# Issuing the experts' down-projection weights from ScalarE's DMA queue

## The chip, the cores and the metric

The kernel runs on one core of a Trainium2 chip. The metric is device time in microseconds (us) of one execution. Times of the kernel before are the median of three runs, and one further execution was taken with the hardware profiler; its rows stand below.

Engines are named as the profile names them: PE is TensorE's matmuls, PEld its weight loads, DVE is VectorE, ACT is ScalarE, POOL is GpSimd, SP is SyncE, which only issues transfers. A "q" behind an engine (SPq, ACTq) is its sequencer, where DMA issues are recorded. Among the DMA queues, q1 carries what SP issues, q10 what ACT issues and q0 what POOL issues.

## What is computed

One decoder layer on 4096 tokens of width 512, in float32: a Mamba-2 mixer, cross attention to a context of 77 rows, then a slot mixture of experts. Its feed-forward part is what this change touches. Each of 16 experts works on its own slot row, 2 rows (one per sequence):

```
h = layernorm(o)                       # o: 16 slot rows per sequence, from attention over x
u = silu(einsum('besd,edf->besf', h, W1) + b1)      # W1: 16 x 512 x 2048
g = silu(einsum('besd,edf->besf', h, Wg) + bg)      # Wg: 16 x 512 x 2048
y = einsum('besf,efd->besd', u * g, W2) + b2        # W2: 16 x 2048 x 512
o = o + y
out = mha(x, o, o, ...)                # the combine stage, over all tokens
```

So each expert needs three matrices of 4 MB, 12 MB in all, for very little arithmetic, and 16 experts need 201 MB.

## The kernel before

The program has three large parts: the token stages (mixer, cross attention, attention of slots to tokens), the expert stage, and the combine stage. The parts are separated by who needs what; the expert stage is a loop over 16 experts, `experts(eng, body)`, which every engine runs for itself: experts 0 and 1 written out, a hardware loop over experts 2 to 13 in steps of two, experts 14 and 15 written out. Engines meet only by semaphores.

**Units and ring.** The weights of one expert are cut into 6 units of 2 MB: units 0 and 1 are W1, 2 and 3 are Wg (these four are the up projections' units), 4 and 5 are W2 (the down projections' units). They land in a ring of 6 slots in SBUF, all of 128 partitions x 4096 floats. `slot_of(unit, e)` gives the slot; from expert 2 on, a unit takes the slot that the same unit of the expert before had. The units of expert 0 are fetched during the token stages from ACT's queue, units 0 to 2 of expert 1 go to three spare places at the end of the token stages, so 87 units are left for the expert stage. (In this text "(e,u)" is unit u of expert e.)

**A W1 or Wg unit** is copied as 128 rows of 16 KB, **a W2 unit** as 256 rows of 8 KB (`fetch_unit`, L839 and L842).

**Who waits for what.** PE's `expert` runs, for w = 0 (W1) and 1 (Wg): 16 matmuls on each of two units (L1538), then bias matmuls (L1545). ACT's `activate` takes the silu of each (L1583), DVE multiplies them (L1574), PE transposes the product (L1550), DVE copies it (L1577), and PE runs the down projection on units 4 and 5 (L1560). PE waits for `ring_in` of the unit's slot, and when its last matmul on a unit is done it counts `unit_used` of the slot up (`release`). SP's `stream` waits for `unit_used` of the slot and issues the next unit for it. SP does this in the order 0, 1, 2, 3, 4, 5 of each expert:

```
for unit in range(UNITS):
    if isinstance(e, int) and e == 1 and unit < EXTRA:
        continue
    slot = slot_of(unit, e)
    sp.wait_ge(unit_used[slot], uses(unit, e))
    fetch_unit(sp, io, ring[:, slot, :], ring_in[slot], e, unit)
```

After the last expert's units SP waits for unit (15,0) to be used and issues three loads of 512 KB for the combine stage into its slot (L1871 twice, L1876), rows of 2 KB. POOL issues two bias loads of 8 KB per expert. After the last down projection a chain of small matmuls and copies makes the combine stage's matrices, all engines meet in a barrier, and the combine stage starts at 1430.7 us of the span.

Of the kernel before, what the change touches and what calls it, by code (L numbers as in the profile page):

```python
# [48 lines left out]
UNITS = 6  # L49
# [3 lines left out]
def broadcast(ap, shape):  # L53
    return ap.broadcast_to(shape)
# [89 lines left out]
def wait_later(eng, sem, value):  # L144

    if not isinstance(value, int) or value > 0:
        eng.wait_ge(sem, value)
# [686 lines left out]
def fetch_unit(sp, io, dst, arrived, e, unit):  # L834

    kind, half = unit // 2, unit % 2
    if kind < 2:
        src = (io["e_W1"], io["e_Wg"])[kind].rearrange("e (p k) f -> e p (k f)", p=P)[bass.ds(e, 1), :, half * UNIT:(half + 1) * UNIT]
        sp.dma_start(dst, src.rearrange("o p f -> (o p) f")).then_inc(arrived, 16)  # L839
    else:  # L840
        src = io["e_W2"].rearrange("e (q p s) n -> e p q (s n)", q=4, p=P)[bass.ds(e, 1), :, 2 * half:2 * half + 2, :]
        sp.dma_start(dst.rearrange("p (q n) -> p q n", q=2), src.rearrange("o p q n -> (o p) q n")).then_inc(arrived, 16)  # L842
# [10 lines left out]
def tokens_stage(nc, io, hold, ring, ring_in):  # L853
    with Stage(nc, "mix", hold["arena"], PROJ1_AT) as mt:
        hold["banks"] = mt.banks(4)
        hold["score_banks"] = mt.stack.enter_context(nc.psum_tensor("mix_scores", [P, HG, 512], F32))
        first = mixer_parts(nc, io, hold, mt)
        with Stage(nc, "crs") as st, Stage(nc, "exp") as et:
            slots = expert_parts(nc, io, hold, ring, ring_in, et)
            cross_rows(nc, io, hold, ring, ring_in, st, first, slots)  # L860
# [586 lines left out]
def expert_parts(nc, io, hold, ring, ring_in, st):  # L1447
# [29 lines left out]
    slot, dbo, ln_g, ln_b = (rows[:, i, :] for i in range(4))  # L1477
# [19 lines left out]
    unit_used = [st.sem(f"unit_used{i}") for i in range(UNITS)]  # L1497
# [3 lines left out]
    def slot_of(unit, e):  # L1501

        return unit if isinstance(e, int) and e == 0 else (unit + UNITS - EXTRA) % UNITS

    def uses(unit, e):

        return e - 1 if unit < EXTRA and not (isinstance(e, int) and e == 0) else e
# [71 lines left out]
    def activate(act, e):  # L1579
        wait_later(act, s["gu_done"], e)  # L1580
        for w, dst in ((0, up), (1, gate)):
            act.wait_ge(s["up_done"], 2 * e + w + 1)
            nc.scalar.activation(dst[:], bank[w][:], ACT.Silu).then_inc(s["silu_done"], 1)  # L1583

    def experts(eng, body):

        for e in (0, 1):
            body(e, e, 0)
        with eng.Fori(1, EXPERTS // 2 - 1) as i:
            for u in (0, 1):  # L1590
                body(2 * i + u, u, i)
        for e in (EXPERTS - 2, EXPERTS - 1):
            body(e, e % 2, e // 2)
# [4 lines left out]
    def fetch_rows(sp):  # L1598
        sp.dma_start(dbv[:], io["d_bv"]).then_inc(s["dbv_in"], 16)
        sp.dma_start(rows, io["slot_rows"][:, 0:4, :]).then_inc(s["rows_in"], 16)  # L1600
        sp.dma_start(b2, io["slot_rows"][:, 4, :]).then_inc(s["rows_in"], 16)

    def stream(sp):
        def combine_weights(dst, src, layout):
            sp.dma_start(dst[:], src.rearrange(layout, p=P)).then_inc(s["comb_w_in"], 16)

        for dst, src in ((cbk, io["c_bk"]), (cbv, io["c_bv"]), (cbq, io["c_bq"])):
            sp.dma_start(dst[:], src).then_inc(s["comb_w_in"], 16)
        sp.wait_ge(s["zn_turned"], BATCH * SM)
        combine_weights(cwo, io["c_Wo"], "(k p) n -> p k n")  # L1610
        sp.wait_ge(s["ao_done"], 1)
        combine_weights(cwk, io["c_Wk"], "(p k) n -> p k n")
        combine_weights(cwv, io["c_Wv"], "(p k) n -> p k n")
        sp.wait_ge(s["wo_done"], 1)
        combine_weights(cwqT, io["c_WqT"], "(k p) n -> p k n")

        def step(e, u, half):
            if isinstance(e, int) and e == 0:
                return
            for unit in range(UNITS):  # L1620
                if isinstance(e, int) and e == 1 and unit < EXTRA:
                    continue
                slot = slot_of(unit, e)
                sp.wait_ge(unit_used[slot], uses(unit, e))
                fetch_unit(sp, io, ring[:, slot, :], ring_in[slot], e, unit)
            if isinstance(e, int) and e == 1:
                sp.dma_start(cbo[:], broadcast(io["c_bo"].rearrange("(o n) -> o n", o=1), [P, D])).then_inc(s["comb_w_in"], 16)
        experts(sp, step)

        sp.wait_ge(unit_used[slot_of(0, EXPERTS - 1)], EXPERTS - 1)  # L1630
        fetch_turned(sp, io, hold, 0, 0)
        fetch_turned(sp, io, hold, 1, 1)
        fetch_tokens(sp, io, hold, 0, 0)
# [126 lines left out]
                                 ACT.Copy).then_inc(s["znT_done"], 1)  # L1760

    def activate_all(act):
        experts(act, lambda e, u, half: activate(act, e))
        act.wait_ge(s["k4_done"], 1)
        nc.scalar.activation(k4[:], bank[6][:], ACT.Copy).then_inc(s["k4_out"], 1)
        for k in range(KC):
            act.wait_ge(s["m2_done"], k + 1)
            nc.scalar.activation(hold["m2"][:, :, k, :].rearrange("p b (g r) -> p g b r", g=GROUPS),
                                 bank[k][:].rearrange("p (g b r) -> p g b r", g=GROUPS, b=BATCH), ACT.Copy).then_inc(s["m2_out"], 1)
        act.wait_ge(s["kb_done"], 1)  # L1770
        nc.scalar.activation(hold["kb2"][:].rearrange("p b g r -> p g b r"), bank[6][:].rearrange("p (g b r) -> p g b r", g=GROUPS, b=BATCH),
                             ACT.Copy, scale=SCALE).then_inc(s["m2_out"], 1)
# [10 lines left out]
    def normalise(dve):  # L1783
# [71 lines left out]
        for i in range(BATCH * SM):  # L1855
# [3 lines left out]
                                           ALU.mult, ALU.add).then_inc(s["vo_out"], 1)  # L1859

    return dict(fetch_extra=fetch_extra, fetch_rows=fetch_rows, stream=stream, constants=constants, biases=biases, turn_tokens=turn_tokens,
                multiply=multiply, take_tokens=take_tokens, activate=activate_all, invert_sums=invert_sums, divide_tokens=divide_tokens,
                normalise=normalise, keep_busy=keep_busy)

# [4 lines left out]
def fetch_turned(sp, io, hold, i, u):  # L1869

    sp.dma_start(hold["x2T"][u][:].rearrange("p t k n -> p t (k n)"),  # L1871
                 io["x2T"].rearrange("(t p) n -> p t n", p=P)[:, bass.ds(i * T2, T2), :]).then_inc(hold["x2T_in"][u], 16)


def fetch_tokens(sp, io, hold, i, u):
    sp.dma_start(hold["x2"][u][:], io["x2"].rearrange("(t p) n -> p t n", p=P)[:, bass.ds(i * T2, T2), :]).then_inc(hold["x2_in"][u], 16)  # L1876
# [322 lines left out]
```

## Time and profile before

| | us |
|---|---|
| median of 3 runs | 1575.49 (1572.14 to 1576.46) |
| the profiled execution, its own time | 1573.41 |
| its span in the trace | 1571.8 |
| expert stage in the span | 964.4 to 1410.8 |
| PE busy over the whole span | 1376.2 (88%) |
| DVE, ACT, POOL busy | 803.4, 449.4, 235.4 |

The profile is of one execution. The time of that execution is 1.6 us above its span. Busy time of PE counts matmuls in flight, also when they are spread thinly; in the expert stage the engine-by-engine busy shares are low except for the DMA engines.

### The profile page before, as it was taken

How to read it: one execution, taken by the hardware profiler on the slowest of the kernel's cores; microseconds unless marked ns; L12 is line 12 of the kernel's file. 1: busy time of each engine (PE TensorE's matmuls, PEld its weight loads, DVE VectorE, ACT ScalarE, POOL GpSimd, SP SyncE). 2: the span in 40 equal slices, each digit the busy share in tenths (PEclk: the TensorE clock that was granted, in tenths of full speed). 3: DMA queues.
4: the chain of work that ended last, by engine and by line, in shares of the span. 5: the costliest groups of instructions: out<-in, count | busy, mean ns of one | idle time of the engine just before them, and what ended most of it. 6: DMA issues, size and time to landing. Idle time of an engine off the chain costs nothing. (4 is left out here: it accounts for less than half of the span.)

```text
span 1571.8 us, 26619 instructions
## 1 busy us (share of the span) xinstructions
PE 1376.2 (88%) x10011; PEld 866.8 (55%) x10011; DVE 803.4 (51%) x2195; ACT 449.4 (29%) x938; POOL 235.4 (15%) x214
## 2 busy tenths in 40 slices
PE   6899999999999999999999989856666666678996
PEld 3777777777677777777777755211111111126663
DVE  0646676767777676767676753000000000004997
ACT  2434434334144444444444431000000000002332
POOL 1111111011022121212222221000000000001221
PEclk9899999999999999999999999998988998889998
DMA  9342233122211421153111156999999999972663
GB/s 355 122 147 80 69 95 95 53 82 81 81 56 61 158 105 58 43 192 125 47 53 47 47 210 265 415 426 424 427 426 423 426 427 424 426 298 68 201 201 134
DMA packets 75259, 309.28 MB, mean 197 GB/s; under 512 B 9692, under 2 KB 14940, under 8 KB 57513
## 3 DMA queue, kind: packets, MB, share of 16 engines
q1 hardware_dynamic: 71720, 293.23, 48.5%
q10 hardware_dynamic: 2432, 14.68, 2.7%
q8 instruction: 53, 0.87, 0.2%
q0 software_dynamic: 1024, 0.27, 0.1%
q14 instruction: 30, 0.24, 0.1%
HBM read 274.33 MB, written 33.82 MB: 196 GB/s over the span
## 5 line engine op out<-in xcount | busy, mean ns | idle before, releaser
L1538 PE MATMUL mix_scores<-all_ring,all_space 128*32 128x512 f32 x976 | 146.0, 709 | 102.1 <-DMA all_ring<-in_e_W 53.9
L1574 DVE TENSOR_TENSOR all_space<-all_space 128x512 f32<-128x512 f32 x16 | 11.1, 694 | 396.6 <-ACT all_space L1583 396.6
L175 PE MATMUL mix_bank<-all_ring,all_space 128*128 128x256 f32 x672 | 156.8, 387 | 2.1 <-POOL all_ring L1419 2.1
L1538 PEld LDWEIGHTS mix_scores<-all_ring,all_space 128*32 128x32 f32 x976 | 29.9, 118 | 205.2 <-DMA all_ring<-in_e_Wg 79.2
L175 PEld LDWEIGHTS mix_bank<-all_ring,all_space 128*128 128x128 f32 x672 | 126.6, 192 | 28.6 <-issue 9.0
L1583 ACT ACTIVATE all_space<-mix_scores 128x512 f32<-128x512 f32 x32 | 19.1, 597 | 428.7 <-PE mix_scores L1545 428.7
L1151 POOL TENSOR_TENSOR all_space<-all_space 128x1232 f32<-128x1232 f32 x32 | 72.2, 2257 | 396.4 <-DVE all_space L1113 396.4
L1560 PE MATMUL mix_scores<-all_ring,all_space 128*32 128x512 f32 x512 | 114.6, 657 | 15.7 <-DVE all_space L1577 12.6
L930 PE MATMUL mix_bank<-all_space 128*128 128x128 f32 x1024 | 119.8, 275 | 0.0
L969 PE MATMUL mix_bank<-all_space 128*128 128x512 f32 x256 | 117.6, 603 | 0.8 <-ACT all_space L1034 0.8
L930 PEld LDWEIGHTS mix_bank<-all_space 128*128 128x128 f32 x1024 | 116.9, 192 | 0.7 <-issue 0.5
L245 DVE SCALAR_TENSOR_TENSOR all_ring<-all_ring,all_space 128x256 f32<-128x256 f32 x192 | 84.4, 482 | 53.0 <-ACT all_ring L194 50.4
L756 PE MATMUL mix_scores<-all_space,all_ring 128*128 128x512 f32 x240 | 105.5, 592 | 0.8 <-DVE all_ring L806 0.8
L1080 DVE TENSOR_REDUCE all_space<-mix_scores 128x16 f32<-128x1232 f32 x30 | 43.3, 1442 | 93.8 <-PE mix_scores L943 93.8
L1560 PEld LDWEIGHTS mix_scores<-all_ring,all_space 128*32 128x32 f32 x512 | 27.6, 119 | 91.1 <-issue 66.1
L756 PEld LDWEIGHTS mix_scores<-all_space,all_ring 128*128 128x128 f32 x240 | 45.5, 190 | 52.0 <-issue 50.2
L969 PEld LDWEIGHTS mix_bank<-all_space 128*128 128x128 f32 x256 | 47.0, 194 | 48.5 <-issue 48.4
L1028 ACT ACTIVATE all_space<-all_space 128x1232 f32<-128x1232 f32 x32 | 39.4, 1231 | 113.0 <-DVE all_space L1082 113.0
L950 PEld LDWEIGHTS mix_scores<-all_ident,all_space 128*77 128x77 f32 x512 | 58.2, 148 | 18.6 <-issue 15.4
L1052 ACT ACTIVATE all_space<-mix_scores 77x512 f32<-77x512 f32 x128 | 65.3, 588 | 7.1 <-PE mix_scores L950 6.7
L228 POOL TENSOR_TENSOR all_ring<-all_ring,all_dwv 128x512 f32<-128x512 f32 x24 | 30.5, 1272 | 243.8 <-ACT all_dwv L214 242.5
L1058 ACT ACTIVATE all_space<-all_space 128x512 f32<-128x512 f32 x32 | 26.1, 816 | 143.1 <-DVE all_space L641 143.1
(282 smaller groups left out, 2292.0 us busy)
## 6 DMA issues: line engine op xcount, KB each, us to landing
all_ring<-in_e_W SPq DMA_DIRECT2D x58, 2048.0 KB, 26.3
all_ring<-in_e_Wg SPq DMA_DIRECT2D x29, 2048.0 KB, 27.3
all_ring<-in_xT SPq DMA_DIRECT2D x8, 1024.0 KB, 7.7
all_ring<-scratch_rates SPq DMA_DIRECT2D x64, 128.0 KB, 4.2
all_z<-in_x SPq DMA_DIRECT2D x16, 512.0 KB, 4.5
all_space<-scratch_x SPq DMA_DIRECT2D x32, 256.0 KB, 2.8
scratch_x<-all_space SPq DMA_DIRECT2D x32, 256.0 KB, 2.0
scratch_x2T<-all_space SPq DMA_DIRECT2D x32, 256.0 KB, 2.0
```

Source lines behind the costliest of these rows:

```text
L175: last = nc.tensor.matmul(bank[:, i * BT:(i + 1) * BT], hold["win"][:, k, m * P:(m + 1) * P], hold["xT"][b % 2][:, k, :], start=(k == 0), ...
L245: last = nc.vector.scalar_tensor_tensor(conv[:, m0 + i, :], proj[:, m0 + i, k:k + BT], taps[:, m0 + i, k:k + 1], conv[:, m0 + i, :], ALU.m ...
L756: last = nc.tensor.matmul(outputs(c)[b], yT[:, b, g * P:(g + 1) * P], wout[:, g, :], start=(g == 0), stop=(g == GROUPS - 1))
L930: last = nc.tensor.matmul(AV[:, g * P:(g + 1) * P], wq[:, k, g * P:(g + 1) * P], x1T[:, k, :], start=(k == 0), stop=(k == KC - 1))
L950: last = nc.tensor.transpose(SC[0:CTX, g, h * P:(h + 1) * P], pr[:, h * GROUPS + g, :], hold["ident"][:])
L969: last = nc.tensor.matmul(TO[:], yT[:, k, :], wo[:, k, :], start=(k == 0), stop=(k == KC - 1))
L1028: nc.scalar.activation(pr[:], pr[:], ACT.Exp, scale=SCALE).then_inc(s["exp_done"], 1)
L1052: nc.scalar.activation(prT[:, g * HG:(g + 1) * HG, :].rearrange("p h t -> p (h t)"), SC[0:CTX, g, :], ACT.Copy).then_inc(s["prT_done"], 1)
L1080: nc.vector.tensor_reduce(top[:].rearrange("p (i h) -> p i h", i=HG), src, AX.X, ALU.max).then_inc(s["top_done"], 1)
L1151: nc.gpsimd.tensor_tensor(pr[:], pr[:], broadcast(rden[:].unsqueeze(2), [P, HEADS, CTX]), ALU.mult).then_inc(s["normed"], 1)
L1538: last = nc.tensor.matmul(bank[w][q * ROWS:(q + 1) * ROWS, :], hm[u][:, k, :], weights[:, at:at + FQ], start=(k == 0), stop=False)
L1560: last = nc.tensor.matmul(bank[3][q * ROWS:(q + 1) * ROWS, :], guT[:, i, q * ROWS:(q + 1) * ROWS], weights[:, (j * 4 + i) * D:(j * 4 + i + ...
```

## The change

The loop over a unit's wait and fetch becomes a helper, `refill`, that any issuing engine can call. SP's stream now issues units 0 to 3 of each expert from 1 on. Units 4 and 5 of each expert from 1 on are issued by ACT, at the start of its step for that expert, ahead of its waits for the silu. Nothing else moves; the waits on `unit_used`, the slots and the sizes are the same.

```
+    def refill(eng, e, unit):
+        slot = slot_of(unit, e)
+        eng.wait_ge(unit_used[slot], uses(unit, e))
+        fetch_unit(eng, io, ring[:, slot, :], ring_in[slot], e, unit)
+
     def stream(sp):
...
-            for unit in range(UNITS):
+            for unit in range(UNITS - 2):
                 if isinstance(e, int) and e == 1 and unit < EXTRA:
                     continue
-                slot = slot_of(unit, e)
-                sp.wait_ge(unit_used[slot], uses(unit, e))
-                fetch_unit(sp, io, ring[:, slot, :], ring_in[slot], e, unit)
+                refill(sp, e, unit)
...
     def activate_all(act):
-        experts(act, lambda e, u, half: activate(act, e))
+        def step(e, u, half):
+            if not (isinstance(e, int) and e == 0):
+                for unit in (UNITS - 2, UNITS - 1):
+                    refill(act, e, unit)
+            activate(act, e)
+        experts(act, step)
```

On SP, this is one piece of the difference, the end of the second expert's step in the loop over experts 2 to 13. `exp_unit_used1` and `exp_unit_used2` are the slots of units 4 and 5.

```order
 L839 DMA all_ring<-in_e_Wg 128x4096 [waits exp_unit_used5]
 L839 DMA all_ring<-in_e_Wg 128x4096 [waits exp_unit_used0]
-L842 DMA all_ring<-in_e_W 128x2x2048 [waits exp_unit_used1]
-L842 ISA [waits exp_unit_used2]
-L842 DMA all_ring<-in_e_W 128x2x2048
 L1589 REGISTER_ALU
 L1589 COMPARE_AND_BRANCH
```

SP goes from unit 3 of one expert straight to unit 0 of the next, and no longer waits for the down projection's slots.

On ACT, this is the step of expert 0, the step of expert 1 and the start of the loop. Semaphores are printed by the name of their first owner: `tab_tables_ready` is here `up_done` (PE has finished an up projection) and `tab_rates_turned` is `gu_done` (DVE has multiplied).

```order
 L1583 ACTIVATE all_space<-mix_scores 128x512 [waits tab_tables_ready] x2
+L842 DMA all_ring<-in_e_W 128x2x2048 [waits exp_unit_used1]
+L842 DMA all_ring<-in_e_W 128x2x2048 [waits exp_unit_used2]
 L1583 ACTIVATE all_space<-mix_scores 128x512 [waits tab_tables_ready,tab_rates_turned]
 L1583 ACTIVATE all_space<-mix_scores 128x512 [waits tab_tables_ready]
 L1589 UNCONDITIONAL_BRANCH
 L1589 ISA
+L842 ISA [waits exp_unit_used1]
+L842 DMA all_ring<-in_e_W 128x2x2048
+L842 ISA [waits exp_unit_used2]
+L842 DMA all_ring<-in_e_W 128x2x2048
```

ACT's two issues for an expert stand between the second silu of the expert before and the first silu of its own.

## Rows read from the trace of the kernel before

**Rows 1.** The page's slices, 39.3 us each: PE and DMA busy, GB/s.
```profile
PE   6899999999999999999999989856666666678996
DMA  9342233122211421153111156999999999972663
GB/s 355 122 147 80 69 95 95 53 82 81 81 56 61 158 105 58 43 192 125 47 53 47 47 210 265 415 426 424 427 426 423 426 427 424 426 298 68 201 201 134
```

**Rows 2.** Busy time by stretch: the full stage, and three stretches at its end.
```profile
core 0: us, PE busy (x) PEld busy (x) DVE busy (x) ACT busy (x) POOL busy (x), PEclk, DMA share, GB/s
1000.00:1390.00 390.00, 259.87 (x1544) 64.76 (x1538) 22.84 (x50) 15.53 (x26) 13.02 (x25) 0.89 1.01 425
1403.00:1407.00 4.00, 4.00 (x12) 0.94 (x14) 0.00 (x0) 0.00 (x0) 0.00 (x0) 0.59 0.15 58
1407.00:1411.00 4.00, 4.00 (x24) 1.10 (x20) 0.14 (x1) 0.00 (x0) 0.11 (x1) 1.00 0.06 22
```

**Rows 3.** Waits between 1000 and 1360 us: total, times, longest.
```profile
PEld mix_scores L1538 <- DMA all_ring<-in_e_Wg: 67.1, 23, 3.9
PEld mix_scores L1538 <- DMA all_ring<-in_e_W: 56.8, 17, 3.9
PEld mix_scores L1560 <- DMA all_ring<-in_e_W: 8.9, 10, 2.1
```

**Rows 4.** DMA issues: count, KB each, median us from issue to landing.
```profile
all_ring<-in_e_W SPq DMA_DIRECT2D x58, 2048.0 KB, 26.3
all_ring<-in_e_Wg SPq DMA_DIRECT2D x29, 2048.0 KB, 27.3
```

**Rows 5.** Timeline, an expert in mid-stage at reduced clock: start, duration, engine, line.
```profile
1337.53 3.20 PE L1538 MATMUL mix_scores<-all_ring,all_space 128*32 128x512 f32 x16 [2.97 <-DMA all_ring<-in_e_Wg]
...
1344.99 7.00 PE L1560 MATMUL mix_scores<-all_ring,all_space 128*32 128x512 f32 x32 [0.79 <-DVE all_space L1577]
...
1350.27 2.13 SPq L842 DMA_DIRECT2D all_ring<-in_e_W  x2
```

**Rows 6.** Timeline, an expert near the start, at full clock.
```profile
1035.89 1.92 PE L1538 MATMUL mix_scores<-all_ring,all_space 128*32 128x512 f32 x16 [2.97 <-DMA all_ring<-in_e_Wg]
...
1041.66 3.63 PE L1560 MATMUL mix_scores<-all_ring,all_space 128*32 128x512 f32 x16 [0.78 <-DVE all_space L1577]
...
1045.32 5.33 SPq L842 DMA_DIRECT2D all_ring<-in_e_W  x2
```

**Rows 7.** Timeline, the last expert: unit 3 arrives, down projection, what follows.
```profile
1397.21 1.92 PE L1538 MATMUL mix_scores<-all_ring,all_space 128*32 128x512 f32 x16 [1.61 <-DMA all_ring<-in_e_Wg]
...
1402.98 7.84 PE L1560 MATMUL mix_scores<-all_ring,all_space 128*32 128x512 f32 x32 [0.79 <-DVE all_space L1577]
...
1407.19 0.14 PEld L1560 LDWEIGHTS mix_scores<-all_ring,all_space 128*32 128x32 f32 x6 [0.29 <-DMA all_ring<-in_e_W]
...
1410.75 0.49 PE L1714 MATMUL mix_bank<-all_ident,all_space 128*128 128x128 f32 x2
```

**Rows 8.** DMA view of 547 to 549 us: queue, packets, MB, share.
```profile
DMA packets 87, 0.81 MB, mean 404 GB/s; under 512 B 0, under 2 KB 0, under 8 KB 43
q10 hardware_dynamic: 44, 0.72, 98.0%
q1 hardware_dynamic: 43, 0.09, 11.2%
```

**Rows 9.** The same view of 706 to 708 us.
```profile
DMA packets 161, 0.85 MB, mean 426 GB/s; under 512 B 0, under 2 KB 0, under 8 KB 76
q10 hardware_dynamic: 85, 0.70, 82.4%
q1 hardware_dynamic: 76, 0.16, 19.9%
```

**Rows 10.** Timeline, the start of the expert stage: PE, ACT's silu, SP's issues.
```profile
964.39 3.64 PE L1538 MATMUL mix_scores<-all_ring,all_space 128*32 128x512 f32 x32 [0.39 <-DVE all_space L1830]
966.38 0.33 SPq L839 DMA_DIRECT2D all_ring<-in_e_Wg  x1
968.09 2.95 SPq L842 DMA_DIRECT2D all_ring<-in_e_W  x2
971.09 0.48 SPq L1627 DMA_DIRECT2D all_space<-in_c_bo  x1
972.53 9.48 SPq L839 DMA_DIRECT2D all_ring<-in_e_W  x2
973.25 0.60 ACT L1583 ACTIVATE all_space<-mix_scores 128x512 f32<-128x512 f32 x1 [3.69 <-PE mix_scores L1545]
983.25 8.06 SPq L839 DMA_DIRECT2D all_ring<-in_e_Wg  x2
```

**Rows 11.** Issues at L842 on ACT's queue, duration in ns and where.
```profile
L842 ACTq DMA_DIRECT2D all_ring<-in_e_W x2: 381/383/385, 701.3 to 717.1; - x2
```

## The prediction, made before the changed kernel ran

> **What bounds the kernel now.** I read the page's slices first [rows 1]. In most of the span PE is busy in nine tenths of a slice and the DMA engines in one to four. From slice 26 to 35 it is the other way round: PE falls to five to eight tenths, the DMA engines stand at nine or more, and the rate is flat at 415 to 427 GB/s. That is the expert stage, the only place the change touches. The view by stretches says the same more sharply [rows 2]: from 1000 to 1390 us the 16 DMA engines are busy for 1.01 of the time at 425 GB/s, at a mean granted PE clock of 0.89. So a 2 MB unit takes 2.097 MB / 425 GB/s = 4.93 us, one expert 29.6 us. The waits show who pays [rows 3]: PE's weight loads wait 67.1 + 56.8 us for W1 and Wg units, and only 8.9 us for W2 units. A unit lands 26 to 27 us after its issue [rows 4], over five unit times, so five to six units are always queued. The queue never runs dry and is served in order, so inside the stage a unit arrives every 4.93 us whatever PE does. The stage's length is its bytes over 425 GB/s, plus what follows the last arrivals.
>
> What follows is in [rows 7]. Unit (15,3) starts PE at 1397.21. Silu, multiply and transposes take until 1402.98, 5.77 us, and the two down units another 7.84 us. Unit (15,5), the last one, is there when PE comes to it at 1407.19 (idle before it 0.29 us). So the end of the stage, 1410.75, is **the arrival of unit 3 plus 13.6 us**; the time in which units 4 and 5 arrive is hidden in that chain. Beside this, the DMA rate at the very end is 58 and then 22 GB/s [rows 2], a share of 0.15 and 0.06, about one engine of 16. One engine runs some 8 us behind the others, and landings go by the last one. It moves the same bytes in both kernels, so I treat it as the clock of the stage.
>
> **The change part by part.** (1) Issue cost: 30 issues leave SP and come to ACT, at 0.38 us each [rows 11]. SP had nothing to do but wait. ACT was idle for most of the stage (15.53 us busy of 390 [rows 2]). Its two issues for an expert wait for slots that the down projection before frees, and PE runs the next up projection only after that, at least 2 x 1.92 us [rows 6] before ACT's silu is wanted. So the silu queued behind the waits is not late: 0. If that cover were gone, it would be 2 x 0.38 us for each of 15 experts, 11 us.
>
> (2) Bytes: the same, at the same 425 GB/s as long as one queue has work. 0, with bounds below.
>
> (3) **Order of arrival: the term that counts.** Before, one queue served 0, 1, 2, 3, 4, 5. Now there are two. How do they share an engine? The token stages show it, where ACT fetched expert 0's units beside SP's 2 KB rows. From 547 to 549 us q10 moved 44 packets (0.72 MB, 16 KB each) and q1 43 packets (0.09 MB, 2 KB each) [rows 8]; from 706 to 708 us, with W2's 8 KB packets, 85 against 76 [rows 9]. So they alternate packet by packet, whatever a packet holds. A W1 or Wg unit gives each engine 8 packets of 16 KB, 4.93 / 8 = 0.616 us each; a W2 unit 16 packets of 8 KB, 0.308 us each. A pair takes 0.924 us, SP gets two thirds of the bytes and ACT one third. SP carries 4 of 6 units, so the two queues use exactly their shares: 32 pairs are 29.6 us, one expert.
>
> Now let x be the W2 packets (of the 32 of its expert) that an engine still has to move when unit 3 has landed. In the kernel before x is 32, units 4 and 5 whole, 9.86 us. In the changed one x shrinks, as W2 is moved beside Wg. The last expert's unit 3 then lands x times 0.308 us before the end of the bytes instead of 9.86 us before it. What bounds x? From below: ACT can issue unit 4 of an expert only when half of the down projection before is done. By the rows that is 9.4 us after unit 3 came to PE at full clock [rows 6] and 12.7 us at reduced clock [rows 5], and I allow 0.9 us more until data moves (my choice; no row shows it). If ACT's queue is just never dry, the leftover is worked off in that time: x = 10.3 / 0.924 = 11 to 13.6 / 0.924 = 15. From above: unit 5 lands x times 0.924 us after unit 3, then PE needs 3.63 us for its half of the down projection, 2 us for unit 0 of the next expert, and 1 us passes to SP's issue; this must fit in 29.6 us for SP's queue to stay filled, so x is at most 24. Between 15 and 24 nothing pulls x either way, so the start decides.
>
> The start [rows 10]: SP issued (1,3), (1,4), (1,5) at 966.4, 968.1 and about 970.6. Now ACT issues (1,4) only after expert 0's second silu ends, 973.85. SP sends (1,3), then (2,0) at 972.5. ACT's queue starts 5 us late, is alone for about 2 us near 981 (SP waits for the down projection's slots), ends (1,5) near 999.5, and has moved only some 6 of expert 2's 32 packets when (2,3) lands near 1005. So x starts at about 26, is pushed under 24 by SP's full ring, and should stay near the top. I take x = 20: unit (15,3) lands 20 x 0.308 = 6.2 us before the end of the bytes instead of 9.86, **+3.7 us**. With x from 15 to 24 it is +5.2 to +2.5.
>
> (4) With a large x, PE gets to the next up projection late. For x = 20 unit 5 lands at 18.5, its half ends at 22.4, and four units back to back (964.39 to 973.2, 8.8 us [rows 10]) end at 31.2, against 29.6 plus the 2.9 us that PE spends on unit 3 and the biases when its arrival decides: no loss at full clock. For x = 24 it is 34.9 against 32.5, +2.4. At a clock of 0.89 a little more. I put **+0.5** (0 to 2.4); it grows as (3) shrinks, so the sum of the two stays between 3.6 and 5.5.
>
> (5) Start gap: between the end of (1,3) near 972 (with 0.7 us of the small load behind it) and the first data of (2,0) near 973.4 the engines stand almost idle, where before (1,4) followed. **+0.5 us** (0 to 1).
>
> (6) At the end SP's three loads of 512 KB now share the engines with units (15,4) and (15,5): packets of 2 KB, about 0.09 us. Twenty W2 packets then take 20 x 0.40 = 8 us after unit 3, and the second half of the down projection wants unit 5 at 10 us (1407.19 - 1397.2 [rows 7]): 0, and 0 for the combine stage, whose first loads land before its start at 1430.7.
>
> Sum: 3.7 + 0.5 + 0.5 = **+4.7 us**. The profiled execution took 1573.41 us (span 1571.8); with the change it would take 1578.1. The median of the runs shown is 2.1 us above the profiled one, so the prediction against it is 1575.5 + 4.7 = 1580.2 us.
>
> **Rivals.**
> - *Even sharing by bytes.* If long packets are cut or taken in bursts, ACT gets half while both have work. Both W2 units then land with or before unit 3, x is between 0 and 11, and unit (15,3) lands 0 to 3.4 us before the end of the bytes: +6.4 to +9.9, with the start gap about +8.7, 1584 us. Against it stand [rows 8] and [rows 9], where packet counts match and bytes don't. The Trainium skill (DMA: Bandwidth & Descriptors, "Queues, rings and completion order") says an engine drains a whole packet of some 9 to 17 descriptors before it turns to the next ring; if a turn were so long, a turn would be a unit's whole share on either queue, which is this rival. The packets in this trace are single rows, so I hold it for the less likely.
> - *Two streams cost rate.* Two places of HBM read in turn, one engine already lagging. 1% of 434 us of streaming is +4.3 on top, 1584.5. For it: 404 GB/s in [rows 8]; against it: that is beside 2 KB packets, and [rows 9] shows 426.
> - *Two streams gain rate (the other side).* If an engine overlaps one ring's packet with the other's, each packet may cost less. 425 would have to become 430 to pay the 4.7 us back; 435 would give -10 + 4.7 = -5.5, 1570 us. Against it: the share is 1.01 already [rows 2], and in the mixed stretches the sum of both queues is 404 to 426, never above [rows 8, 9]. The same page of the Trainium skill ("Issuing engines are not separate DMA queues") says that spreading issues over engines saves only sequencer time; no run here shows it yet for two large streams.
> - *Nothing moves that can be measured.* x stays at its top, PE is not late, and the lagging engine's tail hides the rest: +2 to +3, 1578 us.
>
> **How the numbers follow.** About 0.3%, 4.7 us, is what a measurement of this kernel can tell from no change; my likeliest case lies on that line. Packet sharing as worked out (sum 3.6 to 6.5): 0.58. Even bytes 0.10, lost rate 0.12, gained rate 0.08, nothing that shows 0.12. Of the likeliest case somewhat over half counts as slower, with the two dearer rivals 0.53; the rest of it, the fourth rival and half of the gain make 0.40 the same; 0.07 faster. The likeliest case's own range is 1578.5 to 1582. For eight in ten I go from 1574.5 (part of the gained rate) to 1586.5 (the dear rivals with the 1 to 2 us by which runs differ).
>
> **What would show it.** In mid-stage: the two queues' packet counts equal, 425 GB/s and share 1.01 as before; W2 units about 30 us from issue to landing at most; PE waiting for W2 units (L1560) as well as for W1 and Wg; unit 5 landing 14 to 22 us after unit 3. At the end: the last expert's L1538 on unit 3 starts 3 to 5 us later than 1397.2, and L1714 follows it by 13.6 us as before. The even-bytes rival would show no waits at L1560 and unit 3 as the last to land. It is wrong if the rate in the stage differs by 1% either way, if ACT's issues last much over 0.38 us (a full queue) and delay its silu, or if the end of the stage no longer hangs on unit 3.

## The result, and the profile after

The change made the kernel slower, by well under 1%. Four runs gave a median of 1585.24 us (1583.03 to 1589.16), against 1574.9 us before (1572.14 to 1576.46); the ratio (after over before) is 1.0067, 95% interval 1.0053 to 1.008. Timed again later on another occasion, seven runs gave 1585.11 us against 1576.14 us, ratio 1.0057 (1.0036 to 1.0078). So the loss is 9 to 10 us where I forecast 4.7. The direction held, and the measured 1585.24 us lies in the range of 1574.5 to 1586.5; the forecast size was half of the measured one.

The profiled execution took 1589.16 us (span 1587.6), 3.9 us above the median. The page's slices, as in [rows 1], with the granted clock added:

```profile
PE   6899999999999999999999989776676677678996
PEclk9899999999999999999999999987888878878999
DMA  9342233222211421152111058999999999952553
GB/s 345 131 143 83 65 94 94 69 65 81 87 54 55 166 94 59 53 207 95 59 40 59 34 207 309 423 425 427 424 425 426 425 420 414 428 213 66 199 199 133
```

The stage is still flat at the DMA engines' rate. The page's DMA queues and issues, answering to [rows 4]:

```profile
q1 hardware_dynamic: 63560, 230.31, 38.6%
q10 hardware_dynamic: 10592, 77.60, 12.3%
...
all_ring<-in_e_W ACTq DMA_DIRECT2D x34, 2048.0 KB, 18.6
all_ring<-in_e_Wg SPq DMA_DIRECT2D x29, 2048.0 KB, 26.2
```

The view by stretches, answering to [rows 2]:

```profile
core 0: us, PE busy (x) PEld busy (x) DVE busy (x) ACT busy (x) POOL busy (x), PEclk, DMA share, GB/s
1000.00:1360.00 360.00, 253.47 (x1408) 67.27 (x1404) 21.45 (x48) 14.33 (x24) 13.00 (x25) 0.83 1.01 424
1421.40:1444.70 23.30, 18.03 (x101) 12.07 (x99) 6.73 (x15) 3.66 (x7) 0.99 (x2) 0.85 0.00 1
```

The first row is the middle of the stage: the same share and nearly the same rate (425 before), but a PE clock of 0.83 where the same stretch had 0.89. The second is the chain behind the last down projection. In the first profile of before it looks like this:

```profile
1411.00:1430.70 19.70, 14.43 (x98) 9.97 (x98) 6.60 (x15) 3.63 (x7) 0.88 (x2) 0.99 0.00 1
```

The same work took 3.3 us longer at the lower clock. The waits between 1000 and 1360 us, answering to [rows 3]:

```profile
PEld mix_scores L1560 <- DMA all_ring<-in_e_W: 50.4, 12, 6.5
PEld mix_scores L1538 <- DMA all_ring<-in_e_Wg: 49.7, 12, 6.3
```

PE now waits once per expert for unit 3 (L1538) and once for unit 5 (L1560), and no longer for units 0 to 2. The timeline of the last two experts, answering to [rows 5] and [rows 7]:

```profile
1377.27 3.47 PE L1538 MATMUL mix_scores<-all_ring,all_space 128*32 128x512 f32 x16 [3.44 <-DMA all_ring<-in_e_Wg]
...
1384.58 3.63 PE L1560 MATMUL mix_scores<-all_ring,all_space 128*32 128x512 f32 x16 [0.79 <-DVE all_space L1577]
1388.25 10.52 ACTq L842 DMA_DIRECT2D all_ring<-in_e_W  x2
...
1392.03 4.49 PE L1560 MATMUL mix_scores<-all_ring,all_space 128*32 128x512 f32 x10 [3.82 <-DMA all_ring<-in_e_W]
...
1407.00 2.97 PE L1538 MATMUL mix_scores<-all_ring,all_space 128*32 128x512 f32 x16 [2.64 <-DMA all_ring<-in_e_Wg]
1409.72 1.76 PE L1545 MATMUL mix_scores<-all_space 128*32 128x512 f32 x8
...
1414.46 7.05 PE L1560 MATMUL mix_scores<-all_ring,all_space 128*32 128x512 f32 x32 [0.79 <-DVE all_space L1577]
1421.44 0.49 PE L1717 MATMUL mix_bank<-all_ident,all_space 128*128 128x128 f32 x2
...
1424.83 1.94 PE L1728 MATMUL mix_bank<-all_dwv,all_space 128*32 128x512 f32 x8 [0.47 <-DVE all_space L1851]
```

Read it so: PE starts on (14,3) at 1377.27 and on (14,5) only at 1392.03, 14.8 us later, and behind that it runs the next expert's units, which have landed meanwhile, back to back. In the following I call such a stretch of several units in a row a burst. L1728 takes 1.94 us here; the same eight matmuls took 1.06 us in the first profile of before (L1725 there), so they ran at about half speed.

**Where the time went.** This execution reached the expert stage 4.9 us later than the first one of before (969.25 against 964.39), ahead of anything the change touches; the next profile of the same program began it at 960.96. So I count from the stage's first L1538. Two profiles of the changed kernel and three of the kernel before (the later ones are told of below) give:

| us | before, three profiles | changed, two profiles | difference of means |
|---|---|---|---|
| first L1538 to PE's start on (15,3) | 432.8, 432.6, 432.5 | 437.8, 439.2 | +5.9 |
| from there to the end of the last down projection | 13.5, 13.4, 13.4 | 14.4, 14.9 | +1.2 |
| from there to the combine stage's first matmul | 19.95, 19.96, 22.88 | 23.23, 23.15 | +2.3 |
| combine stage | 141.1, 141.0, 142.7 | 142.9, 142.9 | +1.3 |

In all +10.7 us, in keeping with 9 to 10 in the medians. The first line is the arrival of the last unit that the up projections need. In the other three, 4.8 us, PE waits for no weight unit in the changed kernel; they are the same instructions at a lower PE clock. Below, "+439.2" means 439.2 us after the stage's first L1538, and "the chain" is the third line.

### The profile page after: what moved, and what is told of

It reads as the page before. It is cut to its first block and busy times, and to the rows that moved or that the text cites. A ratio compares the mean times of both kernels' runs of the same rounds, so it can differ in the third digit from the quotient of the medians.

```text
span 1587.6 us, 26633 instructions
## 1 busy us (share of the span) xinstructions
PE 1404.1 (88%) x10011; PEld 881.1 (56%) x10011; DVE 804.0 (51%) x2195; ACT 450.3 (28%) x938; POOL 235.1 (15%) x214
## 5 line engine op out<-in xcount | busy, mean ns | idle before, releaser
L1538 PE MATMUL mix_scores<-all_ring,all_space 128*32 128x512 f32 x976 | 171.6, 685 | 45.7 <-DMA all_ring<-in_e_Wg 45.3
L1560 PE MATMUL mix_scores<-all_ring,all_space 128*32 128x512 f32 x512 | 151.5, 764 | 59.4 <-DMA all_ring<-in_e_W 46.8
L1560 PEld LDWEIGHTS mix_scores<-all_ring,all_space 128*32 128x32 f32 x512 | 32.9, 135 | 165.0 <-issue 89.9
L930 PE MATMUL mix_bank<-all_space 128*128 128x128 f32 x1024 | 119.8, 275 | 0.0
L1538 PEld LDWEIGHTS mix_scores<-all_ring,all_space 128*32 128x32 f32 x976 | 39.1, 119 | 129.2 <-issue 68.6
L1028 ACT ACTIVATE all_space<-all_space 128x1232 f32<-128x1232 f32 x32 | 39.3, 1230 | 113.8 <-DVE all_space L1082 113.8
L998 PE MATMUL mix_bank<-all_space 128*128 128x128 f32 x512 | 67.3, 285 | 0.1
```

The source lines that it names most:

```text
L930: last = nc.tensor.matmul(AV[:, g * P:(g + 1) * P], wq[:, k, g * P:(g + 1) * P], x1T[:, k, :], start=(k == 0), stop=(k == KC - 1))
L998: last = nc.tensor.matmul(slot_bank(t)[:, m * P:(m + 1) * P], hold["m1"][:, k, m * P:(m + 1) * P], x2T[u][:, k, :], start=(k == 0), stop=( ...
L1538: last = nc.tensor.matmul(bank[w][q * ROWS:(q + 1) * ROWS, :], hm[u][:, k, :], weights[:, at:at + FQ], start=(k == 0), stop=False)
L1560: last = nc.tensor.matmul(bank[3][q * ROWS:(q + 1) * ROWS, :], guT[:, i, q * ROWS:(q + 1) * ROWS], weights[:, (j * 4 + i) * D:(j * 4 + i + ...
```

## The experiments

Each ratio is against the median of the kernel before, timed on the same occasion.

**The changed kernel again.** No edit.

> The changed kernel as it is, timed again with a second profile. Reading of the first profile: unit (15,3) reaches PE 4.9 us later after the start of the expert stage (437.8 instead of 432.8 us), and PE's clock is lower around and behind the end of the stage, which costs another 4 to 6 us. Theory A (arrival order and clock are both systematic): unit 3 again 4 to 6 us later counted from the stage's first L1538, the clock over the span 0.940 to 0.945 against about 0.957, the stretch from the last down projection's end to the combine stage's first L1927 again 2 to 4 us longer than 19.9 us, time 9 to 11 us above the kernel before. Theory B (only the order is systematic, the clock was this execution's chance): unit 3 the same 5 us later, clock back at 0.955, time 4 to 6 us above.

Measured: 1585.11 us, ratio 1.0057 (1.0036 to 1.0078), the clock over the span 0.943 in the median of its runs, 0.954 in those of the kernel before. (15,3) came at +439.2 us, the stretch behind the down projection took 23.15 us. Theory A: both parts come again.

**The last expert's W2 back on SP.**

```
-            for unit in range(UNITS - 2):
+            last = isinstance(e, int) and e == EXPERTS - 1
+            for unit in range(UNITS if last else UNITS - 2):
...
-            if not (isinstance(e, int) and e == 0):
+            if not (isinstance(e, int) and e in (0, EXPERTS - 1)):
```

> The changed kernel, but the last expert's units 4 and 5 are issued by SP behind its unit 3, as before; experts 1 to 14 keep both queues. If the late arrival of (15,3) is the order of arrival alone, it reaches PE 432 to 434 us after the stage's first L1538 instead of 437.8, and the time falls by 4 to 5 us against the changed kernel. If what costs is something in the steady state of two queues (rate, start gap), it stays at 437 to 438. The clock in the stage should stay at the changed kernel's 0.84 in both theories, since the PE bursts of experts 2 to 14 are as in the changed kernel; if the clock is what is left, the time is still 4 to 6 us above the kernel before.

Measured: 1577.6 us, ratio 1.0012 (0.9996 to 1.0028), so 7.5 us of the changed kernel's 9 came back, by the place of two transfers out of 30. (15,3) was no longer waited for, since PE came to it late: (14,5) is still late (PE starts on it at 1387.84 us of the span), and PE runs four units back to back behind it, as step (4) of the prediction describes for a large x. The transposes began 441.0 us after the first L1538, 4.0 later than before and 3.6 earlier than the mean of the two changed profiles; the down projection then ran without a stop and ended at 448.3, 4.8 us before the mean of the two changed profiles. The chain behind it took 19.96 us, at a mean clock of 0.98, though the middle of the stage stood at 0.83:

```profile
1000.00:1360.00 360.00, 246.79 (x1396) 65.64 (x1398) 21.44 (x48) 14.33 (x24) 12.98 (x25) 0.83 1.01 422
```

But the spells at low clock had not gone, they had moved: the combine stage took 144.3 us here, more than the 141.0 to 142.9 of the five profiles in the table. Chain and combine stage together are 164.3 us, against 166.2 and 166.0 in the changed kernel and 161.1, 161.0 and 165.6 in the kernel before.

So the order of arrival in the last expert is what costs most: of the 7.5 us, 4.8 are the earlier end of the stage and some 1.8 the clock behind it. The clock in mid-stage doesn't decide the clock of the chain. My expectation for this run was 4 to 5 us of gain, which is what the end of the stage gave; I had not counted the clock that comes back with it.

**Rows of 4 KB for W1 and Wg, on two queues and on one.** These two and the next two runs copy other rows of the same matrices, so each expert multiplies permuted weights; bytes, units, waits and instruction counts stay.

```
-        src = (...)[kind].rearrange("e (p k) f -> e p (k f)", p=P)[bass.ds(e, 1), :, half * UNIT:(half + 1) * UNIT]
-        sp.dma_start(dst, src.rearrange("o p f -> (o p) f")).then_inc(arrived, 16)
+        src = (...)[kind].rearrange("e (k p) (c n) -> e p c k n", p=P, c=2)[bass.ds(e, 1), :, half, :, :]
+        sp.dma_start(dst.rearrange("p (k n) -> p k n", k=4), src.rearrange("o p k n -> (o p) k n")).then_inc(arrived, 16)
```

> The changed kernel with W1 and Wg units copied as 512 rows of 4 KB from other places of the matrix (so the numbers that the experts multiply are permuted; sizes, counts and waits are the same). Theory packets (an engine alternates packet by packet): a pair is 4 KB for SP and 8 KB for ACT, ACT gets two thirds while both have work, W2 units land in some 7 to 12 us, PE no longer waits at L1560, and unit 3 is the last to land: unit (15,3) reaches PE 9 to 11 us later than in the kernel before (442 to 444 us after the stage's first L1538), so some 4 to 5 us slower than the changed kernel, if 4 KB packets cost no rate. Theory bytes (both queues share bytes evenly): nothing changes against the changed kernel, 437 to 439 us.

> The kernel before with W1 and Wg units as 512 rows of 4 KB (operands permuted): partner of the earlier 4 KB run with two queues, where unit (15,3) reached PE 454.9 us after the stage's first L1538, 22 us later than in the kernel before. Theory packets: 10 us of that are the order (all of W2 landed before unit 3) and 12 us are the rate of 4 KB packets; here, on one queue, unit (15,3) comes at 443 to 446 and the bytes end at 453 to 455, time 10 to 13 us above the kernel before. Theory bytes: the order is worth only 5 us there as well, so the rate must be 17 us, and unit 3 comes at 449 to 451 here.

Measured: on two queues 1602.18 us (ratio 1.0166, 1.0142 to 1.0191) with (15,3) at +454.9; on one queue 1591.78 us (1.0094, 1.0078 to 1.011) with (15,3) at +445.4. The order is worth 9.5 us here, as the theory of packets says; the bytes theory wanted 5. The time, however, fell 17 us behind the changed kernel instead of 4 to 5, since 4 KB rows cost 12 us in themselves (413 GB/s in mid-stage on one queue, 164 ns a packet). The one-queue run was 15 us above the kernel before where I had 10 to 13: its chain took 23.09 us and its combine stage 142.9, although PE takes the units there as they land. The DMA view of 8 us of the two-queue run, in which both queues have work:

```profile
q10 hardware_dynamic: 283, 2.18, 65.4%
q1 hardware_dynamic: 283, 1.16, 36.2%
```

283 packets each, and two thirds of the engines' time for ACT's larger ones. Equal counts alone don't say how many packets an engine takes from one queue before it turns. The end of the changed kernel's first profile does, from 1410.9 to 1412.4 us, where ACT's 8 KB rows run beside SP's 2 KB rows:

```profile
DMA packets 8, 0.04 MB, mean 27 GB/s; under 512 B 0, under 2 KB 0, under 8 KB 4
q10 hardware_dynamic: 4, 0.03, 5.2%
q1 hardware_dynamic: 4, 0.01, 1.4%
```

A share of 6.6% is one engine of 16, and in the packet records its eight packets alternate, one row of ACT and one of SP every 0.39 us. So a turn is one row. In the 4 KB run with two queues PE no longer waited at L1560, only for unit 3 (waits between 1000 and 1360 us):

```profile
PE mix_scores L1538 <- DMA all_ring<-in_e_Wg: 126.9, 17, 12.0
```

**Rows of 8 KB, on two queues and on one.** As above with `"e (c k p) n -> e p c k n"` and k=2, so that all packets are alike.

> The changed kernel with W1 and Wg units copied as 256 rows of 8 KB, as W2's are (so the numbers that the experts multiply are permuted). To be read against the next run, which has the same rows on one queue. Theory packets: both queues' packets are 8 KB, so they share evenly while both have work, few W2 packets are left when unit 3 has landed (0 to 12), and unit (15,3) reaches PE 7 to 11 us later after the stage's first L1538 than in its one-queue partner (16 KB rows: 4.9 and 6.4 us in two profiles; 4 KB rows: W2 all landed, so about 10 to 12). Theory bytes: the same distance as with 16 KB rows, 5 to 6 us.

> The kernel before with W1 and Wg units as 256 rows of 8 KB (operands permuted). Partner of the run above: the price of the packet size alone. In the 4 KB run a packet took 164 ns where a quarter of a 16 KB one is 154, so smaller packets cost rate. With W2's 8 KB packets at 314 ns against half of 616, I expect the bytes to end 4 to 6 us later than with 16 KB rows, unit (15,3) at 436 to 439 us after the stage's first L1538, and a time 4 to 6 us above the kernel before, in every theory.

Measured: on two queues 1588.22 us (1.0075, 1.0055 to 1.0096) with (15,3) at +442.4; on one 1583.72 us (1.0044, 1.0028 to 1.0059) with (15,3) at +437.0. The queues do share evenly, 223 packets against 221 in 8 us:

```profile
q10 hardware_dynamic: 223, 1.70, 51.2%
q1 hardware_dynamic: 221, 1.69, 50.6%
```

But the order is worth 5.4 us, under the 7 to 11 that I expected. In mid-stage W2 was indeed all landed when unit 3 came (ACT's queue stood empty from about 1352 to 1361 us); in the last expert ACT issued only at 1391.6, so its queue still had some packets when (15,3) landed. The size of this case alone would not have told the theories apart (the bytes theory had 5 to 6 us), nor do its packet counts, since equal rows share evenly under both; the 4 KB pair does. On one queue (15,3) came where I had put it (436 to 439), but the time was 7 us above the kernel before instead of 4 to 6: here too the chain and the combine stage were slow, 21.6 and 143.0 us, without any longer bursts.

**Longer bursts of PE on one queue.** The kernel before, with one wait more on PE:

```
     def expert(pe, e, u, half):
         pe.wait_ge(s["hm_done"], e + 1)
         wait_later(pe, s["silu_done"], 2 * e)
+        if not (isinstance(e, int) and e < 2):
+            unit_of(pe, e, 2)
```

> The kernel before with one wait more: from expert 2 on PE waits for unit 2 of an expert before it starts unit 0, so units 0, 1 and 2 run back to back behind each other, as they do in the changed kernel. All transfers stay on SP's queue in their old order. Theory clock (PE's longer bursts lower its granted clock, and that costs behind the stage): mean clock in the stage falls from 0.89 to 0.84 to 0.86 and over the span from 0.957 to 0.94 to 0.95, unit (15,3) arrives as before (432 to 434 us), and the time is 3 to 5 us above the kernel before. Theory B (order of arrival is all): clock and time as in the kernel before, within 2 us.

Measured: 1580.97 us, ratio 1.0029 (1.0015 to 1.0044), 4.8 us above the kernel before. Mean clock over the span 0.930, in mid-stage 0.79 at an unchanged 425 GB/s:

```profile
1000.00:1360.00 360.00, 216.23 (x1392) 60.05 (x1392) 21.44 (x48) 14.34 (x24) 12.98 (x25) 0.79 1.01 425
```

The last down projection ended at +448.2 (1.8 to 2.3 us later than before, since PE has three units to run when it starts), the chain behind it took 23.27 us and the combine stage 142.9. So PE's own grouping of the work costs about 5 us with every transfer where it was; some 2 of them are the later end of the down projection, and the rest lies behind the stage. The clock fell further than I expected, to 0.79.

**Bursts everywhere but in the last expert, and in the last two alone.** The added wait is left out for the last expert as well in the one, and stands only for experts 14 and 15 in the other:

```
+        if not (isinstance(e, int) and (e < 2 or e == EXPERTS - 1)):     # the one
+        if isinstance(e, int) and e >= EXPERTS - 2:                      # the other
```

> The earlier experiment with PE's longer bursts on one queue, but the last expert starts unit 0 as soon as it lands, as in the kernel before. Clock in the stage stays at about 0.78 to 0.80. Theory recent (what PE does in the last 30 us sets the half-speed spells behind the stage): the stretch from the last down projection's end to the combine stage's first matmul is 20 us again, not 23.3, and the time is within 2 us of the kernel before. Theory mean (the stage's whole record lowers the clock behind it): 23.3 us and 4 to 6 us above the kernel before, as with bursts everywhere.

> One queue, transfers as in the kernel before, but PE waits for unit 2 before unit 0 only in experts 14 and 15; experts 2 to 13 run as before, so the stage's mean clock stays near 0.89. Theory recent (PE's work in the last 30 to 40 us decides the half-speed spells behind the stage): the last down projection ends 1 to 2 us later, the stretch from there to the combine stage's first matmul is 23 us instead of 20, and the time is 4 to 5 us above the kernel before, as with bursts in all experts. Theory mean: 20 us and within 2 us of the kernel before. The run with bursts everywhere but in the last expert gave 19.96 us and no loss.

Measured: everywhere but in the last, 1576.46 us, ratio 0.9997 (0.9988 to 1.0006). In the last two alone, 1580.14 us, ratio 1.0029 (1.0014 to 1.0044). Mid-stage and the chain behind the stage, first of the one:

```profile
1000.00:1360.00 360.00, 217.25 (x1394) 59.80 (x1392) 21.44 (x48) 14.33 (x24) 12.96 (x25) 0.79 1.01 425
1411.10:1431.00 19.90, 14.68 (x100) 10.19 (x98) 6.74 (x15) 3.59 (x6) 0.99 (x2) 0.98 0.00 1
```

and the timeline of the other, just behind its stage:

```profile
1411.62 0.49 PE L1716 MATMUL mix_bank<-all_ident,all_space 128*128 128x128 f32 x2
...
1415.02 1.94 PE L1727 MATMUL mix_bank<-all_dwv,all_space 128*32 128x512 f32 x8 [0.47 <-DVE all_space L1845]
...
1421.00 5.46 PE L1738 MATMUL mix_scores<-all_space,all_dwo 128*128 128x128 f32 x32 [0.49 <-DVE all_space L1854]
```

A clock of 0.79 through twelve experts cost nothing against the median of the kernel before. Bursts in the last two cost all of the 5 us: the last down projection ended at +448.4 instead of +446.3, and the chain took 23.24 us instead of 19.96, with L1738 at 5.46 us where the kernel before has 3.84. So the chain's clock follows what PE does in the last experts, as theory recent says.

The chain is not the whole bill, though. With bursts everywhere but in the last expert the low clock came some 20 us later, at the start of the combine stage. Its first 15 us, first in this run and then in the first profile of before:

```profile
1431.05:1446.05 15.00, 12.90 (x42) 10.47 (x43) 4.55 (x8) 2.99 (x4) 3.17 (x3) 0.73 0.37 106
1430.70:1445.70 15.00, 12.89 (x53) 10.73 (x54) 4.85 (x9) 3.00 (x4) 4.24 (x4) 0.90 0.34 106
```

42 matmuls against 53 in the same time. Its combine stage took 144.3 us, chain and combine stage together 164.2, against 166.1 with bursts in the last two experts. So of the 5 us, 2 are the late down projection and about 2 the clock; and a short chain alone doesn't show that the clock was not paid.

**Two more profiles of the kernel before.** No edit.

> The kernel before, for a second profile. If the stretches behind the stage (19.95 us and 141.1 us) are its own, they come again within 0.5 and 2 us; if the first profile was a lucky one, one of them is 3 us longer, and the clock's part of the changed kernel's loss is smaller than the 5 us that the first profiles give. Unit (15,3) at 432.5 to 433.5 us after the stage's first L1538.

> A third profile of the kernel before, for the same question: 20 us and 141 to 144 us behind the stage, (15,3) at 432.5 to 433.5.

Measured: 1572.69 us with 19.96 and 141.0 us behind the stage; 1576.86 us with 22.88 and 142.7. So the slower chain is not the changed kernel's alone: the kernel before has it in some executions, and with 2.9 and 1.7 us in the two stretches it accounts for the 4.2 us by which these two executions differ. The changed kernel had it in both of its profiles, and both runs with bursts in the last expert too; but so did the one-queue run with 4 KB rows, in which PE has no longer bursts than before. The clock's price is therefore a matter of how often, and its mean here 3.6 us behind the stage (two profiles against three), not 5. How often the kernel before pays it isn't shown: two of its three profiles are faster than its median on every occasion.

**W1 on ACT's queue instead of W2.**

```
-            for unit in range(UNITS - 2):
+            for unit in range(2, UNITS):
...
-            if not (isinstance(e, int) and e == 0):
-                for unit in (UNITS - 2, UNITS - 1):
+            if not (isinstance(e, int) and e < 2):
+                for unit in (0, 1):
```

> Two queues as in the changed kernel, but the other way round: from expert 2 on ACT issues units 0 and 1 (W1), SP issues 2, 3, 4, 5. The same share of the bytes goes over ACT's queue, but the last expert's W2 stays behind its unit 3 on one queue. Theory order (what is moved in front of unit 3 costs, the second queue as such only the 0.4% that its packets were slower, 1 to 2 us): unit (15,3) reaches PE 432 to 435 us after the stage's first L1538, the bytes end within 2 us of the kernel before, the time is 0 to 4 us above it, the upper half if the half-speed spells fall behind the stage. Theory queue (two streams cost in themselves): unit 3 at 437 to 439 as in the changed kernel and 8 to 10 us above the kernel before.

Measured: 1610.07 us, ratio 1.0213 (1.0189 to 1.0237), the last down projection 475.7 us after the first L1538, 30 us later than before. Neither theory had this. The view by stretches and the timeline of one expert:

```profile
1208.00:1214.00 6.00, 4.71 (x40) 1.00 (x32) 0.59 (x1) 1.19 (x2) 0.62 (x2) 0.94 0.62 210
1214.00:1226.00 12.00, 7.72 (x36) 2.23 (x36) 1.20 (x4) 0.00 (x0) 0.41 (x1) 0.85 1.00 427
```

```profile
1212.78 0.60 ACT L1583 ACTIVATE all_space<-mix_scores 128x512 f32<-128x512 f32 x1 [4.12 <-PE mix_scores L1545]
1212.93 0.85 ACTq L839 DMA_DIRECT2D all_ring<-in_e_W  x2
```

ACT issues the next expert's W1 only behind its second silu, and they land some 15 to 22 us later, beside SP's (PE starts on them at 1227.53 and 1234.94 us). SP meanwhile waits for PE to use units 2 to 5 and its queue runs empty, so in the expert shown the engines stand at 0.62 for 6 us, 210 GB/s. Over the middle of the stage the rate is 396 to 399 GB/s instead of 425. So this run doesn't answer the question that it was made for, what a second queue costs by itself; the run with the last W2 on SP comes closer, with two queues through 14 experts and a time within 0.3% of the kernel before. The change under study escapes this by its choice of units: W2 is wanted last, and SP's queue has the four others.

## Why the prediction was right or wrong

The sum was 4.7 us: 3.7 for the order, 0.5 for PE being late and 0.5 for the start gap. The profiles gave 10.7: 5.9 for the arrival of (15,3), where order and gap had 4.2, and 4.8 in three stretches that the sum left as they were.

*What bounds the stage*: right. 424 GB/s and a share of 1.01 in mid-stage, and the end hangs on unit 3: in both changed profiles PE waits for (15,3), 2.6 and 4.8 us, and the down projection runs through.

*(1) Issue cost 0*: right. ACT's 32 issues at L842 took 375 to 482 ns, the silu was never behind them.

*(2) The same rate*: nearly. 424 and 422 GB/s from 1000 to 1360 us instead of 425; I had 0. How much of it counts is seen at the end: the last W2 packet ended at +443.1 and +444.6 us in the changed kernel, at +442.3, +441.9 and +441.8 in the kernel before, and some 1.3 us of the later end are SP's 2 KB packets between the last W2 ones. That leaves 0 to 1.5 us for the rate and the start gap together.

*(3) Order of arrival*: the mechanism was right, and the term was mis-sized. Packets alternate (283 to 283 with 4 KB rows, and one by one at the end), and the 4 KB pair shows what happens when all of W2 gets in front, 9.5 us. But x was not 20. From expert 3 on unit 5 came 13 to 17 us after unit 3 (14.8 for expert 14), which is x = 14 to 18, the low end. In the last expert the packet records show about 15 and 16 W2 packets left, in the two profiles, on the engine that ends last when (15,3) has landed. The step that failed reads "Between 15 and 24 nothing pulls x either way, so the start decides": at expert 2 the gap was still large, as I had it, but SP's queue stood empty twice around it, for longer than the 2 us that I allowed, and ACT had caught up by expert 3. The DMA views of 987 to 990 us and of 1011 to 1014 us, in the first changed profile:

```profile
q10 hardware_dynamic: 171, 1.28, 100.9%
q1 hardware_dynamic: 2, 0.03, 2.5%
...
q10 hardware_dynamic: 160, 1.23, 98.4%
q1 hardware_dynamic: 5, 0.03, 2.6%
```

In both ACT's rows have the engines almost to themselves. With x = 15 my own list gave +5.2; the two changed profiles gave +4.9 and +6.4 for the arrival, start gap and rate included. So this term was some 1.5 us too small.

*(4) PE late behind unit 5*: seen, as the two-queue run with the last W2 on SP shows (transposes 4.0 us late with no wait for unit 3). In the changed kernel it cost nothing by lateness, but it made PE's bursts, and those I priced only as lateness. In the run with the last W2 on SP the lateness did cost: the stage ended 2.2 us later than before.

*(5) Start gap* (+0.5): not told apart from the rate.

*(6) The end*: right, unit 5 was there, and its packets took 0.39 us each where I had 0.40.

**What was missing is the clock.** I read 0.89 in [rows 2], and used it only to stretch a row. 1.2 us on unit 3 and its biases, 2.3 us in the chain behind the stage and 1.3 us in the combine stage, 4.8 in all, are the term that the sum didn't have. That PE's bursts in the last experts bring it was shown on one queue, at about 2 us behind the stage against the run without them. That it is the same cause in the changed kernel is argued, not shown: it rests on the pattern (same 23.2 us, same rows at half speed) and on the chain's 19.96 us with the last expert's old order. Against it stands that one of three profiles of the kernel before had most of it too, and the one-queue 4 KB run all of it.

*The rivals*: even sharing by bytes is refuted by the packet counts with unequal rows. With it goes, here, a turn of 9 to 17 rows: one engine took 8 KB and 2 KB rows in turn, one by one. The Trainium skill (DMA: Bandwidth & Descriptors, "Queues, rings and completion order") gives 9 to 17 descriptors as typical for a turn; if a row is one descriptor, which no run here shows, the measurement differs from it. Two streams that cost rate: 0.2 to 0.7% by the rates, not 1%. Two streams that gain: no; the same page of the Trainium skill ("Issuing engines are not separate DMA queues") says that issuing from several engines saves only time on the sequencer, and no run here was faster. My range's upper end was built for two of these rivals, and neither came. That it held the result is luck: it held the clock, a cause that I hadn't named.

## What to carry to other kernels

On a saturated DMA path a second queue moves no byte faster, it only changes who arrives before whom; ask which arrival starts the last chain, and keep everything else behind it. How two queues share is set by the size of their rows, not by their bytes, so a queue with small rows is the one that starves. A lower PE clock was free here while transfers bound, and was paid where PE bound again behind them, by about 2 us for bursts in the last experts. So look at what PE does in the last piece before that stretch, not at the mean, and add up all stretches behind it before you call the clock free.

## What the runs showed of the hardware

- Two queues alternate packet by packet on an engine, a packet being one row: 16 KB beside 2 KB 44 to 43, 8 KB beside 8 KB 223 to 221, 8 KB beside 4 KB 283 to 283, and 8 KB beside 2 KB one by one on the engine that ended last.
- Row size costs rate even in 2 MB transfers on one queue: 425 GB/s with W1 and Wg in 16 KB rows, 421 in 8 KB rows, 413 in 4 KB rows (W2 in 8 KB rows throughout).
- One of the 16 engines ended its part of the last W2 unit at +442.3 us in the first profile of before, the others by about +436, and PE's start on the second half of the down projection goes by the last one ([rows 2] and [rows 7] show the same stretch). Why it lags stays open.
- The half-speed spells of PE depend on how its work is grouped: with the same instructions and transfers the clock in mid-stage was 0.89 with units taken as they land and 0.79 with three units at once.
- Where the spells fall behind the stage shifts from run to run: with bursts everywhere but in the last expert the chain stood at 0.98 and the 15 us behind it at 0.73.
